# Weight dequantisation of a four-block transformer kernel moved into the first stage (ticks 5 to 31 in place of 8 to 38)

## What is computed

```python
x = x + _L0_xattn_ref(_layernorm(x), ctx, ctx, Wq, bq, Wk, bk, Wv, bv, Wo, bo)  # autocorrelation attention by FFT, top 4 lags
x = x + _L0_ffn_ref(_layernorm(x), w_freq_real, w_freq_imag, bias)              # one linear map in the frequency domain
x = x + _L1_xattn_ref(_layernorm(x), ctx, ctx, ...)                             # deformable sampling of values
x = x + _L1_ffn_ref(_layernorm(x), w_gate, w_up, w_down)                        # gated FFN, quantised activations and weights

def lpbq_dequant(w):                       # on w_gate, w_up (768 x 256) and w_down (256 x 768)
    wb = w.reshape(O, I // 32, 32)
    s = max(max(abs(wb), axis=-1) / 7, 1e-12)
    return (clip(round(wb / s), -8, 7) * s).reshape(O, I)
```

## Time and profile before

| | before |
|---|---|
| median of 3 runs | 885.82 us |
| lowest, highest | 881.6, 889.68 us |
| the profiled execution | 885.08 us |
| its span, first to last instruction | 883.3 us |
| PE / PEld / DVE / ACT / POOL busy | 86 / 55 / 71 / 53 / 28 % |
| mean granted clock of PE | 0.942 |

### The profile page before, as it was taken

One profiled execution on the slowest core, in us unless ns is written; L12 is line 12 of the kernel. 1 busy time (PEld: TensorE's weight loads), 2 busy tenths in 40 slices (PEclk: granted clock), 3 DMA queues, 4 the chain that ended last, 5 costly groups with the idle time before them and its releaser, 6 DMA issues.

```text
span 883.3 us, 10850 instructions
## 1 busy us (share of the span) xinstructions
PE 758.5 (86%) x3680; PEld 489.1 (55%) x3680; DVE 630.0 (71%) x1170; ACT 465.1 (53%) x818; POOL 249.8 (28%) x198
## 2 busy tenths in 40 slices
PE   4999999789999989966999987999979991029998
PEld 3777777568766667723445453444434440018887
DVE  3467688876678658874799977578659997993333
ACT  2444444555433767765555531433369967944341
POOL 3000000456786102246567731000014320000000
PEclk9999999889999999969999997999999996559999
DMA  8900000032043300000000000000004339701111
GB/s 269 348 7 1 1 1 1 0 92 41 5 137 92 49 1 1 1 0 1 1 1 1 1 1 0 1 0 1 1 40 159 157 143 374 267 0 36 48 47 60
DMA packets 31787, 52.82 MB, mean 60 GB/s; under 512 B 3187, under 2 KB 26995, under 8 KB 30582
## 3 DMA queue, kind: packets, MB, share of 16 engines
q1 hardware_dynamic: 30192, 50.62, 17.4%
q10 hardware_dynamic: 1542, 1.52, 0.6%
HBM read 35.28 MB, written 16.84 MB: 59 GB/s over the span
## 4 chain that ended last, share of the span: by engine, by line
PE 68%; ACT 13%; DVE 10%; issue 5%; DMA 2%; POOL 1%; ACTq 1%; SPq 0%; DVEq 0%; POOLq 0%
PE pair L1496 10%; PE pair L1543 9%; PE pair L1140 7%; PE pair L1144 4%; PE pair L1424 4%; PE pair L1392 4%; PE pair L1407 3%; PE pair L1186 3%; DVE wide L2002 3%; PE pair L1249 3%; PE pair L1293 2%; PE pair L1435 2%; ACT upq L1069 2%; ACT g2q L1075 2%; PE pair L1289 2%
## 5 line engine op out<-in xcount | busy, mean ns | idle before, releaser
L1849 DVE SCALAR_TENSOR_TENSOR hat<-pair,hat 128x1024 f32<-128x1024 f32 x64 | 77.9, 1218 | 31.4 <-ACT hat L958 19.9
L958 ACT ACTIVATE hat<-pair 128x1024 f32<-128x1024 f32 x64 | 65.5, 1024 | 61.5 <-PE pair L1392 61.5
L1521 PE MATMUL pair<-xqs,wuT 128*128 128x512 f32 x192 | 84.7, 601 | 4.8 <-ACT up_stage L1025 4.8
L1496 PE MATMUL pair<-xqs,wgT 128*128 128x512 f32 x192 | 85.7, 604 | 0.0
L1543 PE MATMUL pair<-wdT,hid 128*128 128x256 f32 x384 | 83.1, 379 | 0.4 <-DVE hid L2050 0.4
L712 POOL TENSOR_TENSOR hat<-hat 128x1024 f32<-128x1024 f32 x30 | 70.7, 2358 | 41.2 <-DVE hat L1849 41.2
L1543 PEld LDWEIGHTS pair<-wdT,hid 128*128 128x128 f32 x384 | 72.9, 190 | 11.1 <-DVE hid L2050 1.2
L1521 PEld LDWEIGHTS pair<-xqs,wuT 128*128 128x128 f32 x192 | 36.9, 194 | 51.3 <-issue 51.0
L612 POOL TENSOR_TENSOR rstd<-lnt,half 128x8 f32<-128x8 f32 (+2 forms) x15 | 26.3, 1756 | 133.7 <-DVE lnt L1587 133.7
L1140 PE MATMUL pair<-wT,ft_sb 128*128 128x256 f32 x256 | 63.8, 392 | 0.0
L1090 ACT ACTIVATE hid<-wide,unit 128x768 f32<-128x768 f32 x32 | 32.5, 1026 | 57.2 <-DVE hid L2050 43.7
(11 more groups left out here) (230 smaller groups left out, 1742.3 us busy)
## 6 DMA issues: line engine op xcount, KB each, us to landing
up_far<-up_stage SPq DMA_DIRECT2D x24, 512.0 KB, 2.6
ups<-up_far SPq DMA_DIRECT2D x8, 1536.0 KB, 7.0
x_sb<-in_x_dram SPq DMA_DIRECT2D x8, 512.0 KB, 7.4
c_sb<-in_ctx_dram SPq DMA_DIRECT2D x8, 512.0 KB, 8.4
ctx<-in_ctx_dram SPq DMA_DIRECT2D x32, 128.0 KB
out_dram<-x_sb SPq DMA_DIRECT2D x16, 256.0 KB, 2.1
ctx<-in_ctx_dram SPq DMA_DIRECT2D x16, 126.0 KB
four<-in_c_four_dram SPq DMA_DIRECT2D x1, 1280.0 KB, 9.3
```

The costliest lines, as they stand in the source:

```text
L958: nc.scalar.activation(ramp(n), sides_of(n)[:].rearrange("p i t -> p (i t)"), ACT.Relu).then_inc(relu_done, 1)
L1496: last = mm(bank[2 + oc][:], wgT[:, c, oc * 128:(oc + 1) * 128], xqs[:, s, c, :], start=(c == 0), stop=(c == DC - 1))
L1521: last = mm(bank[2 + oc], wuT[:, c, oc * 128:(oc + 1) * 128], xqs[:, t % 2, c, :], start=(c == 0), stop=(c == DC - 1))
L1849: V.scalar_tensor_tensor(ramp(n), sides_of(n)[:].rearrange("p i t -> p (i t)"), 0.0, ramp(n), ALU.max, ALU.add).then_inc(hat_done, 1)
```

## The change

```diff
--- before.py
+++ after.py
@@ -69,8 +69,7 @@
 EDGE_TICK = S4 + 6
 ZERO_TICKS = [S4 + 23 + k for k in range(8)]
 GW_TICKS = list(range(S4 + 6, S4 + 24, 2))
-DEQ_TICKS = [t for t in range(8, 60) for _ in range(1 if t % 8 in (4, 6, 7) or t < 22 or t >= S3 else 2)
-             if not (t < 22 and t % 8 in (4, 6, 7))][:B]
+DEQ_TICKS = [t for t in range(5, B) for _ in range(2 if t % 8 < 4 and t >= 16 else 1) if t not in (14, 22, 30)][:B]
 HALVES = 2 * NQ
```

## The result

| | before | after |
|---|---|---|
| median of 14 runs each | 883.77 us | 877.0 us |
| lowest, highest | 881.52, 961.7 us | 875.6, 882.72 us |
| ratio of after to before | | 0.992 (95%: 0.9901 to 0.9939) |
| the profiled execution / its span | 885.08 / 883.3 us | 876.13 / 874.3 us |
| mean granted clock of PE | 0.942 | 0.949 |

The change makes the kernel 0.8% faster: by the ratio 7.1 us, with an interval of 5.4 to 8.7 us. The forecast was 7.4 us. The ratio leaves the one run of 961.7 us out. The two profiled executions lie 8.95 us apart, more than the medians, and that is taken apart behind the repeats (e13, e12).

What follows compares the result with a forecast made beforehand. DVE was taken to bound PE in ticks 34 to 40, through seven dequantisation steps. Gaps of 4.7 us less 0.4 staying, plus 3.1 of slow clock, give 7.4 us: 885.82 becomes 878.4 us, range 875 to 883.5.

Steps and rivals of the forecast that it cites:

- The bound was DVE, through the seven steps: Ticks 34 to 40: DVE bounds PE; moving seven steps out of ticks 32 to 38 frees at least 8.4 us.
- The gaps close, 0.4 us stay: Ticks 37 to 39: PE's three `x_sb` gaps, 4.70 us in sum, close except for 0.4, bounds 0 and 0.8.
- The slow clock after the last gap, 3.1 us: After 179.58 us PE's lower clock costs 3.1 us; it stays up after the change, so all is gained.
- The first slow stretch, behind the 3.58 us gap, stays as it is: Tick 34: the gap for ACT's `wcol` and the slow clock behind it stay, since ACT's queue is untouched.
- The sum: Whole kernel: 4.7 us of gaps less 0.4 that stay, plus 3.1 of slow clock, gives 7.4 us.
- Stage 1 hides the rest: Ticks 16 to 19: step pairs make DVE at most 0.7 us late, within `xn`'s cover of 1.18; PE loses nothing.
- The forecast's point from which it would cost: Ticks 16 to 19: DVE overflow ends slower than before from 2.15 us of overrun per tick; chance 0.05.
- `four`: Load issued in tick 43: its matmuls start at about 192.9 us, with its cover of about 1.0 us kept.
- The signs of being wrong: Clock at 0.50 after tick 39, PE waiting for POOL's `mix`, or stage 1 ending later than before.
- The forecast's other sum: Ticks 38 and 39: `mix` stretched 0.42 us each by POOL through the shared port, 7.4 - 0.8 = 6.6 us gained.
- The rival of the clock that falls all the same: After tick 34's gap, small gaps pull the clock down again: gain only 4.3 us, median 881.5; chance 0.13.

Runs made afterwards that it cites:

- e13: The unchanged code of the kernel before, profiled once more; the profiled run took 885.85 us.
- e12: The unchanged code of the kernel after the change, profiled once more; the profiled run took 876.33 us.
- e1: Kernel after, but the last seven dequantisation steps put back into ticks 32 to 38; 883.62 us, ratio 0.9982 to before.
- e2: Kernel before with its stage 1 table kept, the last seven steps moved to ticks 49 to 58; 878.15 us, ratio 0.9912 to before.
- e5: Kernel before with `add_att` put ahead of `roll_dve` and `dequantise` in DVE's queue; 886.22 us, ratio 1.0023 to before.
- e6: Kernel after with `add_att` put ahead of `roll_dve` and `dequantise` in DVE's queue; 879.16 us, ratio 0.9919 to before.
- e8: Kernel before with 3, 1 and 5 throwaway matmuls filling PE's gaps in ticks 37, 38 and 39; 882.88 us, ratio 0.998 to before.
- e7: Kernel after with only the last step put back into tick 38; 879.62 us, ratio 0.9956 to before.
- e4: Kernel after, but three steps per tick in ticks 16 to 19 and none in 5 to 8; 882.9 us, ratio 0.9969 to before.
- e11: Kernel after with its last four steps put into ticks 32 to 35, one each; 880.22 us, ratio 0.995 to before.
- e9: Kernel after with ACT's `roll_act` k = 1 put ahead of `swap_v`, for an earlier `wcol`; 879.27 us, ratio 0.9933 to before.
- e3: Kernel before with 5, 2 and 9 throwaway matmuls in PE's queue in ticks 37, 38 and 39; 884.52 us, ratio 0.9996 to before.

## Why the prediction was right, step by step

It said 7.4 us, range 875.0 to 883.5, most likely within 1%; it is 7.1 us by the ratio and 877.0 us. The median of three runs that it started from was 2.05 us above that of fourteen; the terms of the sum are judged on their own. The cause and the place were right. That the total came out within 0.3 us of the ratio's is in part luck, by the two clock terms below.

- **The bound was DVE, through the seven steps.** Right. e1 brings the gaps back with the steps, e2 takes them away by another way. The only changed thing common to e2 and after is that ticks 32 to 38 are free.
- **The gaps close, 0.4 us stay.** Right in size and in place: 0.20 for `x_sb` and 0.21 for `wrow`, 0.41 in sum, 0.55 in e12. The two late ones are those named, tick 38's `roll_dve` and tick 39's `wrow`. e5 and e6 show that moving `add_att` hands the lateness on to `wrow`.
- **The slow clock after the last gap, 3.1 us.** The mechanism held: the clock is 1.00 from 170 to 190 in after. The size did not. Behind the fifth bias (the one after the last gap) before and after differ by 2.46 us (20.68 and 18.22), to which the new 0.2 for `wrow` is to be added: 2.7, not 3.1. And that was a long draw: the repeats differ by 1.15 (19.35 and 18.20), so 1.35 with `wrow`, and e8 gives the clock 1.1 us against e13. By the repeats 3.1 was too much by 1.7.
- **The first slow stretch, behind the 3.58 us gap, stays as it is.** Wrong, and this was the term that was missing. The gap stayed (3.59), the stretch didn't: the level is back at about 166.2 us in after, 2.9 us behind the first matmul, and at about 169.0 in before, 6.1 behind. The distance to the second bias shrank by 1.45 us (6.65 to 5.20; 6.91 to 5.25 in the repeats). All six profiles with a step in each of ticks 32 to 38 show the long stretch; after, e12, e2, e6 and e7 show the short one, e4 one between. It isn't simply the steps, for e11 has four of them there and the short stretch, and e9 has none and the long one. In before DVE also holds PE up by 0.3 us just there: from L1175 at 163.91 to L1155 at 165.08 it is 1.17 us, against 0.85 in the same place after, and the `sab` that L1155 reads ends at 164.98 (L1654), behind the step of the tick before. Whether such a small wait keeps the clock down was not shown, and why the stretch is shorter stays open.
- **The sum.** In the repeats e13 and e12 the passage gains 1.66 us up to the second bias, 4.11 from there to the fifth, where the gaps were (16.59 - 6.91 against 10.82 - 5.25), and 1.15 behind it: 6.92. Forecast were nothing, 4.3 and 3.1. The total came out right by luck, since the term that was too large (by 1.95 in this count) and the one left out (1.66) nearly cancel.
- **Stage 1 hides the rest.** Right. Its ticks kept their lengths (4.40 us, 4.85 in ticks 18 and 19); the first `wcol` matmul stands 0.4 us later (163.30 for 162.90), which is there from the first matmul of `project` on (16.83 and 17.22 us) and comes from no wait for `xn`; in the repeats it isn't there (163.16 in e13, 163.13 in e12). Predicted was a lateness of at most 0.7 out of a cover of 1.18; measured was 0.36, which leaves 0.82. The forecast overlooked the ticks with `ln_variance`; tick 21 has a cover of 0.17 before and after: a lateness of more than that, still there in tick 21, would have made PE wait. The forecast's point from which it would cost was not reached, and e4 shows that it exists.
- **`four`.** It starts at 192.13, forecast about 192.9, and waits for nothing.
- **The signs of being wrong.** Two of the three can be seen, and neither counts against the mechanism: PE waits 0.35 us for POOL's `mix`, but as long before, and stage 1 ends 0.4 us later in one pair of profiles and no later in the other.
- **The port.** The forecast's other sum, by the port rule of the Trainium skill (SBUF — State Buffer, "SBUF: two separate sides"), was 6.6 by stretched `mix` instructions. The `mix` of ticks 38 and 39 take 0.41 and 0.40 us in after, unstretched. The one stretched on the way to a gap is `hot`, by 0.46 us, and its share can only lie in the 0.4 of gaps that stay.
- **The rival of the clock that falls all the same** is right as a mechanism, though not for this code: in e7 a single gap of 1.62 us was followed by the lower level, little more than the 1.53 of the earlier trace rows that wasn't. The change escapes it by leaving no gap above 0.21 (0.35 in e12) in ticks 36 to 40: with one of the seven steps left there, 3.2 of the 7 us are lost.

## What to carry to other kernels

Work that nobody needs soon belongs where its engine waits anyway, and the slack to look at is that engine's own wait per tick, spent down to zero but not beyond: two steps a tick were free, three cost 4.3 us. When an engine is late at one place, count all that it owes up to there before reordering, since reordering moved the wait from `x_sb` to `wrow` and saved nothing here. Price the clock behind a gap by more than one profile, and take filler matmuls for a test of it, not for a gain: they won 1.8 us where taking the work away won 7.

## What the runs showed of the hardware

- **The lower clock level lasts differently long behind one and the same gap.** Behind 2.58 us: 6.2 us in before, about 3.5 in e13 and e1. Behind 3.6 us, before the first `wcol` matmul: from 2.9 us (after) to 6.3 (e13).
- **The length of a gap doesn't decide alone whether the level falls.** PE waits for `x_sb` once more near 275 us, and this wait differs from run to run. Behind 1.61 us (before at 277.96) and 1.69 (e4 at 274.57) the next group of four matmuls took 2.07 us. Behind 1.64 (e8), 1.72 (e2) and 2.01 (e12) it took 1.13, and so did those after it. Behind 1.99 (e13) the next group took 1.13 and the one after it 2.08, as in e7. The rows of e13:

```profile
277.17 0.26 PE L1247 MATMUL pair<-bias,small 3*128 3x256 bf16 x1 [1.99 <-DVE x_sb L1708]
277.37 1.13 PE L1249 MATMUL pair<-fold,tr_sb 128*128 128x256 f32 x4
...
279.65 2.08 PE L1249 MATMUL pair<-fold,tr_sb 128*128 128x256 f32 x4
```

- **A part of the kernel that no edit touches takes three values.** From the first `w63m` matmul (L1435 in before) to the first of the fourth block (L1496) it is 156.2 to 156.6 us in before, after, e1, e3, e4, e8 and e12, 158.8 to 158.9 in e5, e6, e7 and e13, and 160.0 to 160.2 in e2, e9 and e11. The clock between 390 and 440 us is 1.00 in after and 0.86 in e11. That is up to 3.9 us between single profiles, half of what this change is worth, which is why the passage and the medians are compared here and not whole spans.
